# Layer 0 of a two-layer graph-attention kernel: sums by pairs of tiles, masks in two halves, denominators of eight tiles together, with smaller stage and mask rings

## Chip, cores and metric

One NeuronCore of one Trainium2 chip runs the whole kernel. The metric is the device time in microseconds (us) of one execution; the number quoted for a kernel is the median of several runs. A difference of 0.2% (7 us) is about what a measurement of this kernel can tell from none.

## Reference, cut to what matters

`x` is 8192 x 64, `adj` is 8192 x 8192 int32 (0 or 1, about one in a thousand is 1). Three graph-attention passes follow each other; the kernel calls them layers 0, 1 and 2. Each computes, for every row i, a softmax over the columns j at which the mask is set:

```
# layer 0
scores = (x @ W @ a1)[:, None] + (entity @ W @ a2)[None, :]
e      = leaky_relu(scores, 0.2); e = where(adj > 0, e, -9e15)
h      = softmax(e, axis=1) @ entity_embs + x
x      = layernorm(x + elu(h))
# layers 1 and 2 (two steps of the second module, the same mask)
Wh = h @ W_l;  scores = leaky_relu(u + v.T + c);  scores = where(adj > 0, scores, -9e15)
h  = 0.2 * x + 0.8 * elu(softmax(scores, axis=1) @ Wh)
...
out = layernorm(x + concat(x, h1, h2) @ mlp_w + mlp_b)
```

## The kernel before, in words

**Tiling.** The 8192 rows i are handled in 16 blocks (NB) of 512. For a block, the 8192 columns j go by in 64 tiles (NT) of 128: a tile is a 128 x 512 matrix with j on the partitions and the block's rows along the free axis. So each layer is 16 x 64 = 1024 tiles. Layers run one after the other, and within a layer the blocks b and the tiles t are two nested loops, unrolled on every engine.

**One tile, step by step.** (1) A start of the scores is written to one of five PSUM banks (`eps`, ES = 5) by VectorE (DVE), line 1156; in layer 0, 17 of the 64 tiles of a block (the set ON_ACT) are started by ScalarE (ACT) instead, line 564. (2) TensorE (PE) adds the mask: `mask_scores`, line 754, multiplies a diagonal of -9e15 (`nbig`) with the tile of the inverted mask. For tiles started by ACT it also adds a row of bounds (`mrow`, line 751) first. (3) ACT takes exp into a slot of a ring of probabilities, `probs`, line 577. (4) PE adds the slot to two running sums in PSUM: `main` (line 798) multiplies with the 64 features; tile j goes to the upper or lower half of the columns by its parity, so that two tiles run side by side in two 64-column halves of the array. `denominators` (line 807) sums four tiles side by side in four 32-column quarters. Layer 1 needs no denominators: its features carry a column of their difference.

**Order of PE's work.** PE's instructions run in program order. In layers 1 and 2 the unit is a pair of tiles: after the mask of every second tile, `main` of the pair two back (GROUP 2, LAG 2). In layer 2 `two_quads` sums the denominators of eight tiles together, once in eight tiles, at t % 8 = 3 (DEN 8, DLAG 3). In layer 0 the unit is a quad: after the mask of every fourth tile, `sums` runs two `main` and one `denominators` for the quad one back (GROUP 4, LAG 1). `mask_scores` writes in pieces of 32 columns in layer 0 (four instructions that run side by side) and of 64 columns in layers 1 and 2 (MASK_COLS), and in one piece of 128 columns near steps that use the whole array.

**Rings.** The ring `prob` has eight slots (TS). Layer 2 uses 16: eight more lie in the buffer `mi`, which layer 0 needs for mask units and later layers don't. `probs` waits until the slot it writes has been summed.

**Tails and heads.** While block b runs, the end of block b-1 (its tail: the sums out of PSUM at t = 4 and 5, turning, division, elu, layer norm, the products for the next layer) and the start of block b+1 (its head: counting edges by level on PE, the row bounds on DVE, T_XOR, T_HIST, T_HEAD, T_HEADT, T_ROWS) are spread over fixed values of t, written by hand at the top of the file.

**The mask, made in layer 0.** The adjacency comes in 512 units of 128 x 1024 int32 (512 KB), 32 for a block. A unit is loaded by SyncE's (SP) queue into one of five slots of `stage` (SS = 5), line 401, once unit h - SS has been used; DVE compares it and writes bytes to `mi` (line 995); `mi` holds eight pairs of units (MR = 8). Each pair is turned by a DMA transpose into `nt` (line 414), and each eight units are stored for the later layers (line 431). All of these are issued in order by SP, as `unit` has it. 32 units are made before the first tile, 52 in block 0, and 32 in each block from 1 to 13, one for two tiles; the last 12 fall in block 14. DVE's program has the mask unit (`make_mask`) between the starts of the tiles, and waits there, in order, until the unit has landed. Layers 1 and 2 load the stored masks (line 437).

The lines that SP runs for one unit:

```
def unit(h):
    if h + SS < NU:
        adj_load(h + SS)      # waits for mask unit h
    if h % 2 == 1:
        turn(h)               # waits for mask unit h
    if h % MU == 3 and h > MU:
        store(h // MU - 1)
```

Of the kernel before, what the change touches and what calls it, by code (L numbers as in the profile page):

```python
# [6 lines left out]
ACT = mybir.ActivationFunctionType  # L7
F32 = mybir.dt.float32
# [8 lines left out]
P = 128  # L17
N = 8192
C = 64
HID = 32  # L20
CE = C + 1
NT = N // P
BI = 512
RT = BI // P
NB = N // BI
# [3 lines left out]
MU = UNITS // MV  # L29
MT = NT // MV  # L30
NU = NB * UNITS
MR = 8
PRO = UNITS
AFTER = 20
SS = 5
HB = 32
LV = 16
SPACE = 14
# [66 lines left out]
def build(nc, x, adj, ent, W0, a0, W12, lin_w, lin_b, attn, mlp_w, mlp_b, out):  # L105
    with ExitStack() as ctx:
# [6 lines left out]
        def sem(name):  # L113
            return ctx.enter_context(nc.semaphore(name))
# [8 lines left out]
        mi = sb("mi", [P, MR, 2 * CW], U8)  # L123
# [70 lines left out]
        eps = ps("eps", [P, ES, BI])  # L194
        acc = ps("acc", [P, BI])
        den = ps("den", [P, BI])
        more = mi[:, :, :].rearrange("p s w -> p (s w)").bitcast(F32).rearrange("p (s w) -> p s w", w=BI)
        misc = ps("misc", [P, BI])
        miscb = misc[:, :].bitcast(BF16)

# [44 lines left out]
        s_pair = sem("pair_of_probs_summed")  # L245
        s_main = sem("probs_used")
        s_den = sem("probs_in_denominators")

# [37 lines left out]
        def tile(l, b, j):  # L286
            return (l * NB + b) * NT + j
# [25 lines left out]
        def den_blocks(l, b):  # L313

            return b if l == 0 else (l - 1) * NB + b

        def group(l, b, k):

            return sum(NB * (NT // GROUP[i]) for i in range(l)) + b * (NT // GROUP[l]) + k

        def summed(l, b, j):

            if j < 0:
                l, b, j = (l, b - 1, j + NT) if b else (l - 1, NB - 1, j + NT)
            return group(l, b, j // GROUP[l]) + 1

        def started(l, b, j, on_act):

# [208 lines left out]
        def _(act):  # L537
# [28 lines left out]

            def probs(l, b, j):

                if l < 2 and j % GROUP[l] == 0 and not (l == 0 and b == 0 and j < TS):
                    act.wait_ge(s_main, summed(l, b, j - TS + GROUP[l] - 1))  # L570
                if l == 2 and j % DEN == 0:
                    if b == 0 and j < TS:
                        act.wait_ge(s_main, group(2, 0, 0))
                    elif b or j >= 2 * TS:
                        act.wait_ge(s_den, b * (NT // DEN) + j // DEN - 1)
                act.wait_ge(s_z, tile(l, b, j) + 1)
                nc.scalar.activation(weights(l, j), eps[:, j % ES, :], ACT.Exp,  # L577
                                     bias=v2col[:, j:j + 1]).then_inc(s_p, 1)

            def sums_out(l, b, par):  # L580
                if l:
                    act.wait_ge(s_main, group(l, b, NT // GROUP[l]))
                else:
                    act.wait_ge(s_pair, (b + 1) * (NT // QUAD))
                nc.scalar.activation(acc_s[:, :], acc[:, :], ACT.Copy).then_inc(s_acce, 1)  # L585

            def denominators_out(l, b):
                if l:
                    act.wait_ge(s_den, (b + 1) * (NT // DEN))
                else:  # L590
                    act.wait_ge(s_main, group(l, b, NT // GROUP[l]))
# [99 lines left out]
        def _(pe):  # L691
# [36 lines left out]

            def mask_cols(l, j, head, tail):

                n = GROUP[l]
                first = j // n * n - 1
# [7 lines left out]
                return P if any(first <= t < first + n for t in whole) else MASK_COLS[l]  # L740

            def mask_scores(l, b, j, par, cols):

# [46 lines left out]
            def main(l, b, k):  # L790

                for i in range(2):
                    j = 2 * k + i
                    h = C * i
                    pe.wait_ge(s_p, tile(l, b, j) + 1)
                    if j == 0 and not (l == 0 and b == 0):
                        pe.wait_ge(s_acce, blk(l, b))
                    mm = nc.tensor.matmul(acc[h:h + C, :], feat[:, l % 2, j, 0:C], weights(l, j),  # L798
                                          start=(k == 0), stop=(k == NT // 2 - 1))
                return mm  # L800

            def denominators(l, b, k):

                if k == 0 and not (l == 0 and b == 0):
                    pe.wait_ge(s_dene, den_blocks(l, b))
                for i in range(QUAD):
                    mm = nc.tensor.matmul(den[32 * i:32 * i + 32, :], ones[:, 0:32], weights(l, QUAD * k + i),  # L807
                                          start=(k == 0), stop=(k == NT // QUAD - 1))
                return mm

            def sums(l, b, k):

                if l:
                    main(l, b, k).then_inc(s_main, 1)
                else:
                    main(l, b, 2 * k)
                    main(l, b, 2 * k + 1).then_inc(s_pair, 1)
                    denominators(l, b, k).then_inc(s_main, 1)

            def two_quads(b, g):  # L820
                denominators(2, b, 2 * g)
                denominators(2, b, 2 * g + 1).then_inc(s_den, 1)

            def bounds(l):
                pe.wait_ge(s_colm, l + 1)
# [61 lines left out]
            for l in range(NLAYER):  # L887
# [13 lines left out]
                def body(b, par, head, tail):  # L901
                    for t in range(NT):
                        if tail and t == T_HT:
                            pe.wait_ge(s_h, blk(l, b))
                        wait_started(l, b, t)
                        mask_scores(l, b, t, par, mask_cols(l, t, head, tail))
                        if t % GROUP[l] == GROUP[l] - 1:
                            k = t // GROUP[l] - LAG[l]
                            if k >= 0:
                                sums(l, b, k)  # L910
                            elif tail:
                                sums(l, b - 1, NT // GROUP[l] + k)
                        if l == 2 and t % DEN == DLAG:
                            g = t // DEN - 1
                            if g >= 0:
                                two_quads(b, g)
                            elif tail:
                                two_quads(b - 1, NT // DEN + g)
                        if tail:
                            tail_step(l, b - 1, t)  # L920
                        if b == 0 and t < (NT + 2) // 3:
                            if t == 0:
                                pe.wait_ge(s_cbe, blk(l, 0) + 1)
                            for j in range(3 * t, min(3 * t + 3, NT)):
                                feature_sum(l, j)
                        if b == 0 and l == 1 and t == T_FSUM + 3:
                            pe.wait_ge(s_fs1e, 1)
                            nc.tensor.matmul(misc[:, 0:CE], acc_s[0:C, 0:P], turnw[0:C, :], start=True,
                                             stop=True).then_inc(s_fsum, 1)
                        if head and t == T_HIST[0]:  # L930
                            if tail:
                                pe.wait_ge(s_oe, 4 * blk(l, b))
                            else:
                                pe.wait_ge(s_fsume, l + 1)
                        for m in range(MV if head else 0):
                            if t == T_HIST[m]:
                                count_edges(l, b + 1, m)
                        if head and t == T_FOLD:
                            turn_counts(l, b + 1)
                        if head and t == T_HEADT:  # L940
                            turn_maxima(l, b + 1)
                        if head and t == T_ROWS:
                            spread_maxima(l, b + 1, 1 - par)

                blocks(body)
                for k in range(NT // GROUP[l] - LAG[l], NT // GROUP[l]):
                    sums(l, NB - 1, k)
                if l == 2:
                    two_quads(NB - 1, NT // DEN - 1)
# [343 lines left out]
```

## Time and profile before

| | |
|---|---|
| median of three runs | 3500.31 us (3499.39 to 3500.57) |
| profiled execution | 3499.27 us, span 3497.5 us |
| TensorE clock granted, mean | 0.983 of full |
| busy, share of the span | PE 92%, DVE 82%, ACT 65%, POOL 3% |
| DMA | 578.71 MB, 165 GB/s mean over the span |

The busy share of PE counts matmuls; weight loads (PEld) overlap them. "Share" of the DMA is the time of all packets over 16 engines; packets can overlap, so that it can be over 1. The 1.8 us between the span and the execution's own time lie outside the profile. The granted clock has two levels, 1.2 and 2.4 GHz, shown as 0.5 and 1.0.

### The profile page before, as it was taken

What the parts mean: (1) busy time and instruction counts of PE and PEld (TensorE: products, weight loads), DVE (VectorE), ACT (ScalarE), POOL (GpSimd) and SP (SyncE); (2) the same over time, 40 slices, a digit from 0 to 9 for tenths busy, and PEclk for the clock granted to TensorE, in tenths of its full rate; (3) what the DMA queues carried; (4) which work ended last, traced back from release to release, by engine and by line L of the source; (5) the groups of instructions that cost most, each with busy time, mean ns of one, the idle gap of its engine ahead of it and who ended that gap; (6) DMA issues with size and microseconds to landing.
All of it is one profiled execution on the core that took longest, in us unless ns stands there. A gap on an engine that the chain in (4) does not pass through costs nothing. (4 is left out here: it accounts for less than half of the span.)

```text
span 3497.5 us, 58252 instructions
## 1 busy us (share of the span) xinstructions
PE 3203.8 (92%) x22959; PEld 1152.7 (33%) x22959; DVE 2873.2 (82%) x5283; ACT 2269.0 (65%) x3933; POOL 114.3 (3%) x138
## 2 busy tenths in 40 slices
PE   1679999999999999799999999988999999999998
PEld 0323333333333333333333333334333333333333
DVE  5468888888888875699999999986888888888886
ACT  0247766676776666377777787773666666666665
POOL 0000000000000000000000000000000000000000
PEclk9989999999999999899999999998999999999999
DMA  8999999999999951222222222112111211221210
GB/s 253 283 348 346 341 329 347 336 333 340 343 333 341 333 180 54 85 85 97 76 100 73 100 73 101 72 61 85 69 72 64 90 71 57 86 82 57 85 33 7
DMA packets 414116, 578.71 MB, mean 165 GB/s; under 512 B 294402, under 2 KB 315010, under 8 KB 389266
## 3 DMA queue, kind: packets, MB, share of 16 engines
q1 hardware_dynamic: 409458, 564.40, 50.2%
q0 software_dynamic: 4384, 10.59, 1.0%
q8 instruction: 180, 2.95, 0.4%
q14 instruction: 94, 0.77, 0.1%
HBM read 430.10 MB, written 77.69 MB: 145 GB/s over the span
## 5 line engine op out<-in xcount | busy, mean ns | idle before, releaser
L1156 DVE SCALAR_TENSOR_TENSOR eps<-ua,v8col,cb 128x512 f32<-128x512 f32 x2800 | 1971.3, 754 | 376.3 <-ACT prob L577 238.9
L577 ACT ACTIVATE prob<-eps,v2col 128x512 f32<-128x512 f32 x2560 | 1628.4, 688 | 692.2 <-PE eps L754 678.9
L798 PE MATMUL acc<-prob,feat 128*64 128x512 f32 x5120 | 1303.3, 605 | 6.6 <-ACT acc_s L585 6.6
L754 PE MATMUL eps<-nt,nbig 128*64 128x512 fp8e4 (+2 forms) x6542 | 994.3, 384 | 114.4 <-DVE eps L1156 110.4
L754 PEld LDWEIGHTS eps<-nt,nbig 128*64 128x64 bf16 (+2 forms) x6542 | 329.8, 104 | 956.0 <-DVE eps L1156 612.5
L798 PEld LDWEIGHTS acc<-prob,feat 128*64 128x64 f32 x5120 | 326.2, 137 | 397.9 <-issue 215.0
L577 ACT ACTIVATE mi<-eps,v2col 128x512 f32<-128x512 f32 x512 | 328.0, 686 | 156.7 <-PE eps L754 152.7
L995 DVE TENSOR_SCALAR mi<-stage 128x1024 uint8<-128x1024 int32 x512 | 352.2, 689 | 62.9 <-DMA stage<-in_adj_dram 62.5
L807 PE MATMUL den<-prob,ones 128*32 128x512 f32 x3072 | 397.0, 604 | 0.0
L798 PE MATMUL acc<-mi,feat 128*64 128x512 f32 x1024 | 264.8, 597 | 0.0
L1004 DVE TENSOR_SCALAR edges<-nt 128x2048 int32<-128x2048 int32 x192 | 234.2, 1220 | 31.1 <-PE misc L765 16.3
L765 PE MATMUL misc<-edges,oneh 128*32 128x512 fp8e4 x3072 | 190.8, 390 | 70.6 <-DVE edges L1004 55.8
L564 ACT ACTIVATE eps<-ub,v8col 128x512 f32<-128x512 f32 x272 | 189.4, 696 | 0.0
L807 PEld LDWEIGHTS den<-prob,ones 128*32 128x32 f32 x3072 | 67.1, 108 | 301.0 <-issue 301.0
L765 PEld LDWEIGHTS misc<-edges,oneh 128*32 128x32 bf16 x3072 | 85.0, 98 | 198.3 <-issue 81.1
L807 PE MATMUL den<-mi,ones 128*32 128x512 f32 x1024 | 123.1, 598 | 0.0
L751 PE MATMUL eps<-mrow,onesb 128*32 128x512 bf16 (+1 forms) x800 | 106.5, 379 | 0.0
L633 ACT ACTIVATE hs<-misc 128x512 f32<-128x512 f32 x48 | 28.3, 589 | 93.8 <-PE misc L765 93.8
L798 PEld LDWEIGHTS acc<-mi,feat 128*64 128x64 f32 x1024 | 68.2, 137 | 54.4 <-issue 20.2
L878 PEld LDWEIGHTS misc<-wcat,ht 65*128 65x128 f32 x384 | 52.5, 198 | 77.8 <-issue 49.5
L637 ACT ACTIVATE mrow<-misc 3x512 bf16<-3x512 bf16 x48 | 28.1, 586 | 76.3 <-PE misc L841 76.3
L878 PE MATMUL misc<-wcat,ht 65*128 65x130 f32 (+1 forms) x384 | 69.8, 306 | 6.5 <-ACT pj L624 4.5
(159 smaller groups left out, 1407.1 us busy)
## 6 DMA issues: line engine op xcount, KB each, us to landing
stage<-in_adj_dram SPq DMA_DIRECT2D x512, 512.0 KB, 6.5
nt<-nt_d SPq DMA_DIRECT2D x128, 1024.0 KB, 5.2
nt_d<-nt SPq DMA_DIRECT2D x64, 1024.0 KB, 7.2
ub<-u_d SPq DMA_DIRECT2D x48, 256.0 KB, 5.2
xy_d<-xin POOLq DMA_DIRECT2D x32, 256.0 KB, 3.3
xin<-xy_d SPq DMA_DIRECT2D x32, 256.0 KB, 2.9
nt<-mi SPq DMA_TRANSPOSE x256, 7.2
xin<-in_x_dram SPq DMA_DIRECT2D x16, 128.0 KB, 6.3
```

The lines of the kernel that those rows point to most:

```text
L564: nc.scalar.activation(eps[:, j % ES, :], ub[:, par, :], ACT.Relu, bias=v8col[:, j:j + 1], scale=1.0 - ALPHA).then_inc(s_filla, 1)
L577: nc.scalar.activation(weights(l, j), eps[:, j % ES, :], ACT.Exp, bias=v2col[:, j:j + 1]).then_inc(s_p, 1)
L633: nc.scalar.activation(hs[:, :], misc[:, :], ACT.Copy).then_inc(s_hse, 1)
L751: nc.tensor.matmul(et[c:c + cols, :], onesb[:, c:c + cols], mrow[:, par, :], start=False, stop=False, skip_group_check=True, tile_position ...
L754: mm = nc.tensor.matmul(et[c:c + cols, :], nbig[:, c:c + cols], edge, start=False, stop=True, skip_group_check=True, tile_position=(0, c))
L765: mm = nc.tensor.matmul(misc[s * HB:(s + 1) * HB, :], oneh[:, m * MT + j, :], half_block(edges[:, n % 2, :], m, j), start=(m == 0 and k == 0),
L798: mm = nc.tensor.matmul(acc[h:h + C, :], feat[:, l % 2, j, 0:C], weights(l, j), start=(k == 0), stop=(k == NT // 2 - 1))
L807: mm = nc.tensor.matmul(den[32 * i:32 * i + 32, :], ones[:, 0:32], weights(l, QUAD * k + i), start=(k == 0), stop=(k == NT // QUAD - 1))
L878: mm = nc.tensor.matmul(misc[:, r * WC + w:(r + 1) * WC], ht[:, (2 * i + r) * P:(2 * i + r + 1) * P], wcat[:, l, w:WC], start=True, stop=True)
L995: dv.tensor_scalar(out, src, 0, ONE8, ALU.is_le, ALU.mult).then_inc(s_mask, 1)
L1004: dv.tensor_scalar(edges[:, n % 2, :].bitcast(I32), nt[:, b % 2, m, :].bitcast(I32), EDGE_FLIP, None, ALU.bitwise_xor).then_inc(s_xor, 1)
L1156: dv.scalar_tensor_tensor(eps[:, j % ES, :], ua[:, par, :], v8col[:, j:j + 1], cb[:, par, :], ALU.add, ALU.max).then_inc(s_fill, 1)
```

## The change

In layer 0 `mask_scores` writes in pieces of 64 columns (HALF); `main` runs by pairs with a lag of two pairs; `denominators` runs for eight tiles together, as in layer 2. The ring of probabilities has 12 slots of its own in all layers (TS = 12), counted over all tiles of the kernel, and layer 2 no longer uses `mi`. ACT's wait for a free slot stands before every second tile, in every layer; in layer 0 and 2 it is for the denominators, in layer 1 for `main`. To make room, `mi` has six pairs in place of eight (MR) and `stage` four slots in place of five (SS).

```
-MR = 8
+MR = 6
-SS = 5
+SS = 4
-GROUP = (QUAD, 2, 2)
-LAG = (1, 2, 2)
+PAIRLAG = 2
-TS = 2 * QUAD
-SLOTS = (TS, TS, 2 * TS)
+TS = 3 * QUAD
-MASK_COLS = (32, 64, 64)
+HALF = 64
...
-        def weights(l, j):
-            n = j % SLOTS[l]
-            return prob[:, n, :] if n < TS else more[:, n - TS, :]
+        def weights(l, b, j):
+            return prob[:, tile(l, b, j) % TS, :]
...
             def probs(l, b, j):
-                if l < 2 and j % GROUP[l] == 0 and not (l == 0 and b == 0 and j < TS):
-                    act.wait_ge(s_main, summed(l, b, j - TS + GROUP[l] - 1))
-                if l == 2 and j % DEN == 0:
-                    if b == 0 and j < TS:
-                        act.wait_ge(s_main, group(2, 0, 0))
-                    elif b or j >= 2 * TS:
-                        act.wait_ge(s_den, b * (NT // DEN) + j // DEN - 1)
+                if tile(l, b, j) >= TS and j % 2 == 0:
+                    old, i = divmod(tile(l, b, j) - TS, NT)
+                    ol, ob = divmod(old, NB)
+                    if ol == 1:
+                        act.wait_ge(s_main, pairs(ol, ob, i // 2 + 1))
+                    else:
+                        act.wait_ge(s_den, dens(ol, ob, i // DEN + 1))
                 act.wait_ge(s_z, tile(l, b, j) + 1)
...
-                        if t % GROUP[l] == GROUP[l] - 1:
-                            k = t // GROUP[l] - LAG[l]
+                        if t % 2 == 1:
+                            k = t // 2 - PAIRLAG
                             if k >= 0:
-                                sums(l, b, k)
+                                main(l, b, k).then_inc(s_main, 1)
                             elif tail:
-                                sums(l, b - 1, NT // GROUP[l] + k)
-                        if l == 2 and t % DEN == DLAG:
+                                main(l, b - 1, NT // 2 + k).then_inc(s_main, 1)
+                        if l != 1 and t % DEN == DLAG:
                             g = t // DEN - 1
                             if g >= 0:
-                                two_quads(b, g)
+                                two_quads(l, b, g)
```

## Rows read from the trace of the kernel before

**Rows 1.** Windows: stretch, length, busy PE, PEld, DVE, ACT, POOL, clock, DMA share, GB/s.

```profile
126.00:249.00 123.00, 99.97 (x681) 43.07 (x685) 79.45 (x129) 55.46 (x90) 0.00 (x0) 0.90 1.07 337
249.08:325.43 76.35, 73.14 (x600) 24.52 (x592) 65.11 (x123) 53.59 (x97) 3.26 (x3) 1.00 1.11 341
325.43:1247.03 921.60, 883.01 (x7156) 295.91 (x7157) 783.61 (x1477) 642.80 (x1140) 35.17 (x36) 1.00 1.11 338
1247.03:1322.08 75.05, 73.67 (x604) 24.84 (x606) 52.40 (x101) 53.33 (x96) 2.82 (x3) 1.00 0.43 132
1322.08:1388.24 66.16, 65.97 (x537) 21.49 (x530) 37.44 (x68) 48.96 (x88) 2.81 (x3) 1.00 0.11 43
...
2458.00:3405.00 947.00, 944.62 (x6678) 336.35 (x6670) 799.74 (x1506) 611.30 (x1026) 36.54 (x28) 1.00 0.19 69
```

**Rows 2.** ACT's copy that opens each block (t = 4), 325 to 1248 us.

```profile
L585 ACT ACTIVATE acc_s<-acc x13: 597/597/597, 325.4 to 1247.0; 128x512 f32<-128x512 f32 x13
```

**Rows 3.** ACT's copy that opens each block, layer 2.

```profile
L585 ACT ACTIVATE acc_s<-acc x14: 597/597/598, 2472.9 to 3348.7; 128x512 f32<-128x512 f32 x14
```

**Rows 4.** Groups by line, one layer 0 block: busy, mean ns | idle before.

```profile
L1156 DVE SCALAR_TENSOR_TENSOR eps<-ua,v8col,cb 128x512 f32<-128x512 f32 x47 | 34.8, 755 | 8.3 <-ACT prob L577 8.0
...
L995 DVE TENSOR_SCALAR mi<-stage 128x1024 uint8<-128x1024 int32 x33 | 22.7, 689 | 0.0
...
L754 PE MATMUL eps<-nt,nbig 128*32 128x512 fp8e4 x160 | 12.8, 381 | 2.7 <-DVE eps L1156 2.6
```

**Rows 5.** Timeline of PE in layer 0, away from tail and head.

```profile
643.09 0.40 PE L751 MATMUL eps<-mrow,onesb 128*32 128x512 bf16 x4
643.31 1.23 PE L754 MATMUL eps<-nt,nbig 128*32 128x512 fp8e4 x16
644.47 1.94 PE L798 MATMUL acc<-prob,feat 128*64 128x512 f32 x8
...
647.22 0.40 PE L751 MATMUL eps<-mrow,onesb 128*32 128x512 bf16 x4
...
651.38 0.59 PE L754 MATMUL eps<-nt,nbig 128*32 128x512 fp8e4 x5
```

**Rows 6.** Timeline of PE in layer 2, away from tail and head.

```profile
2467.38 0.62 PE L754 MATMUL eps<-nt,nbig 128*64 128x512 fp8e4 x4
...
2472.66 1.92 PE L807 MATMUL den<-mi,ones 128*32 128x512 f32 x16
2474.52 0.62 PE L754 MATMUL eps<-nt,nbig 128*64 128x512 fp8e4 x4
```

**Rows 7.** Timeline of PE in layer 0, near the head (tiles 51 to 54).

```profile
616.72 0.40 PE L754 MATMUL eps<-nt,nbig 128*32 128x512 fp8e4 x4 [0.91 <-DVE eps L1156]
```

**Rows 8.** Who waited for whom, layer 0 without its first blocks.

```profile
DVE mi L995 <- DMA stage<-in_adj_dram: 0.4, 1, 0.4
```

**Rows 9.** Who waited for whom, block 0.

```profile
DVE mi L995 <- DMA stage<-in_adj_dram: 34.4, 21, 5.1
```

**Rows 10.** DMA in 145 to 198 us (block 0): total, and the loads' issues.

```profile
DMA packets 16105, 18.86 MB, mean 356 GB/s; under 512 B 12567, under 2 KB 12567, under 8 KB 15717
...
stage<-in_adj_dram SPq DMA_DIRECT2D x23, 512.0 KB, 7.0
```

**Rows 11.** DMA in 60 to 100 us (before the first tile).

```profile
DMA packets 13714, 15.15 MB, mean 379 GB/s; under 512 B 10912, under 2 KB 10912, under 8 KB 13458
...
stage<-in_adj_dram SPq DMA_DIRECT2D x20, 512.0 KB, 6.3
```

**Rows 12.** DMA in 859 to 936 us (a steady block).

```profile
DMA packets 23276, 26.03 MB, mean 338 GB/s; under 512 B 18465, under 2 KB 18469, under 8 KB 22757
...
stage<-in_adj_dram SPq DMA_DIRECT2D x32, 512.0 KB, 6.4
```

**Rows 13.** The loads of the adjacency, 327 to 1100 us: time to landing.

```profile
DMA to landing us min/median/max: 3.8/6.5/10.2
```

**Rows 14.** The DMA transposes of the mask, whole kernel: time that one holds SP.

```profile
L414 SPq DMA_TRANSPOSE nt<-mi x256: 1231/2330/5803, 36.5 to 1267.4; - x128
```

More of the change, by code:

```diff
@@ L196, in build @@
         den = ps("den", [P, BI])
-        more = mi[:, :, :].rearrange("p s w -> p (s w)").bitcast(F32).rearrange("p (s w) -> p s w", w=BI)
         misc = ps("misc", [P, BI])
@@ L244, in build @@
         s_p = sem("probs_done")
-        s_pair = sem("pair_of_probs_summed")
         s_main = sem("probs_used")
@@ L315, in den_blocks, with pairs, dens @@
             return b if l == 0 else (l - 1) * NB + b
[L317 to L325, printed above, removed]
+        def pairs(l, b, n):
+            return (l * NB + b) * (NT // 2) + n
+        def dens(l, b, n):
+            return den_blocks(l, b) * (NT // DEN) + n
         def started(l, b, j, on_act):
@@ L567, in probs @@
             def probs(l, b, j):
-                if l < 2 and j % GROUP[l] == 0 and not (l == 0 and b == 0 and j < TS):
-                    act.wait_ge(s_main, summed(l, b, j - TS + GROUP[l] - 1))
-                if l == 2 and j % DEN == 0:
-                    if b == 0 and j < TS:
-                        act.wait_ge(s_main, group(2, 0, 0))
-                    elif b or j >= 2 * TS:
-                        act.wait_ge(s_den, b * (NT // DEN) + j // DEN - 1)
+                if tile(l, b, j) >= TS and j % 2 == 0:
[5 more added lines that the diff above has]
+                        act.wait_ge(s_den, dens(ol, ob, i // DEN + 1))
                 act.wait_ge(s_z, tile(l, b, j) + 1)
-                nc.scalar.activation(weights(l, j), eps[:, j % ES, :], ACT.Exp,
+                nc.scalar.activation(weights(l, b, j), eps[:, j % ES, :], ACT.Exp,
                                      bias=v2col[:, j:j + 1]).then_inc(s_p, 1)
             def sums_out(l, b, par):
[L581 to L584, printed above, removed]
+                act.wait_ge(s_main, pairs(l, b, NT // 2))
                 nc.scalar.activation(acc_s[:, :], acc[:, :], ACT.Copy).then_inc(s_acce, 1)
             def denominators_out(l, b):
[L588 to L591, printed above, removed]
+                act.wait_ge(s_den, dens(l, b, NT // DEN))
                 nc.scalar.activation(den_s[:, :], den[:, :], ACT.Copy).then_inc(s_dene, 1)
@@ L729, in mask_cols @@
             def mask_cols(l, j, head, tail):
-                n = GROUP[l]
-                first = j // n * n - 1
+                first = j // 2 * 2 - 1
                 whole = []
@@ L739, in mask_cols @@
                     whole += [T_FOLD, T_HEADT, T_ROWS]
-                return P if any(first <= t < first + n for t in whole) else MASK_COLS[l]
+                return P if any(first <= t < first + 2 for t in whole) else HALF
             def mask_scores(l, b, j, par, cols):
@@ L797, in main @@
                         pe.wait_ge(s_acce, blk(l, b))
-                    mm = nc.tensor.matmul(acc[h:h + C, :], feat[:, l % 2, j, 0:C], weights(l, j),
+                    mm = nc.tensor.matmul(acc[h:h + C, :], feat[:, l % 2, j, 0:C], weights(l, b, j),
                                           start=(k == 0), stop=(k == NT // 2 - 1))
@@ L806, in denominators, with two_quads @@
                 for i in range(QUAD):
-                    mm = nc.tensor.matmul(den[32 * i:32 * i + 32, :], ones[:, 0:32], weights(l, QUAD * k + i),
+                    mm = nc.tensor.matmul(den[32 * i:32 * i + 32, :], ones[:, 0:32], weights(l, b, QUAD * k + i),
                                           start=(k == 0), stop=(k == NT // QUAD - 1))
                 return mm
[L811 to L822, printed above, removed]
+            def two_quads(l, b, g):
+                denominators(l, b, 2 * g)
+                denominators(l, b, 2 * g + 1).then_inc(s_den, 1)
             def bounds(l):
@@ L906, in body @@
                         mask_scores(l, b, t, par, mask_cols(l, t, head, tail))
-                        if t % GROUP[l] == GROUP[l] - 1:
-                            k = t // GROUP[l] - LAG[l]
+                        if t % 2 == 1:
+                            k = t // 2 - PAIRLAG
                             if k >= 0:
-                                sums(l, b, k)
+                                main(l, b, k).then_inc(s_main, 1)
                             elif tail:
-                                sums(l, b - 1, NT // GROUP[l] + k)
-                        if l == 2 and t % DEN == DLAG:
+                                main(l, b - 1, NT // 2 + k).then_inc(s_main, 1)
+                        if l != 1 and t % DEN == DLAG:
                             g = t // DEN - 1
                             if g >= 0:
-                                two_quads(b, g)
+                                two_quads(l, b, g)
                             elif tail:
-                                two_quads(b - 1, NT // DEN + g)
+                                two_quads(l, b - 1, NT // DEN + g)
                         if tail:
@@ L945, in _ @@
                 blocks(body)
[L946 to L949, printed above, removed]
+                for k in range(NT // 2 - PAIRLAG, NT // 2):
+                    main(l, NB - 1, k).then_inc(s_main, 1)
+                if l != 1:
+                    two_quads(l, NB - 1, NT // DEN - 1)
                 for t in range(NT):
```

## The prediction, made before the changed kernel ran

> **What bounds the kernel now.** I read the windows first, one for each kind of stretch [rows 1]. The reader should compare the busy columns with the length. Layer 0 from 325.4 to 1247.0 us is twelve blocks (13 copies that open a block [rows 2]), so 76.80 us each. PE is busy for 883.0 of 921.6 us (96%), DVE for 783.6 (85%), ACT for 642.8 (70%), and the DMA share is 1.11. Layer 2 does nearly the same arithmetic in 875.8 / 13 = 67.37 us a block [rows 3], with PE at 99.7% and the DMA at 0.19 [rows 1]. So PE sets the pace now, but in layer 0 two others are close behind: DVE, which also makes the mask, and the DMA, which brings 32 units a block. That the DMA keeps up is seen in the waits: in 773 us DVE waited for a landed unit once, for 0.4 us [rows 8]. In block 0, where 52 units are due in one block, it waited 21 times for 34.4 us [rows 9], and the block takes 123 us between copies [rows 1]. There the DMA is the bound.
>
> **Part 1: PE's order.** Away from tail and head, two quads of layer 0 go from 643.09 to 651.38 = 8.29 us [rows 5]; they hold eight masks and three rows of bounds, each row one more step of 643.31 - 643.09 = 0.22 us. Layer 2's eight tiles by pairs go from 2467.38 to 2474.52 = 7.14 us [rows 6] with no such row. The changed layer 0 should have 7.14 + 3 x 0.22 = 7.80, a gain of 0.49 in eight tiles and 3.9 in 64: 76.8 - 3.9 = 72.9 us a block. The number of products is the same; what goes is the gap at each change of column width. Before, masks (32 columns), `main` (64) and denominators (32) change width twice in four tiles; afterwards twice in eight.
>
> The Trainium skill (TensorEngine Tiling (Array Packing), Key Properties) says that changing the tiling mode drains TensorE. By that rule alone the number of drains halves, from 32 to 16 in a block; the page gives no price for one.
>
> From below, the block is bounded by layer 2's own plus 17 bound rows: 67.37 + 17 x 0.22 = 71.1. From above it is bounded by what DVE holds back: masks in layer 0 stood 2.7 us a block waiting for a start by DVE [rows 4], for instance 0.91 us near the head [rows 7], and that stall does not shrink when PE gets faster; it may grow. DVE would be 65.3 / 73 = 89% busy, with its starts (755 ns) and mask units (689 ns) in one queue [rows 4]. I add 0.6 for it: **73.5 us by PE and DVE**.
>
> **Part 2: the DMA, asked to run faster.** Nothing is taken off it: a block moves 26.03 MB [rows 12]. What it can do when it is the bound is shown twice. In block 0, 23 loads in 53 us at 356 GB/s [rows 10]: 2.30 us a unit, 73.7 us for 32. Before the first tile, 20 loads in 40 us at 379 GB/s [rows 11]: 2.00 us a unit, 64 us for 32, with the engines almost idle. I take 73.7, the stretch that has exp, masks and sums beside it. So the DMA's floor lies right at PE's new pace: most of what PE gains is just allowed, and no more.
>
> The Trainium skill (SBUF — State Buffer, SBUF: two separate sides) says "A DMA cannot be slowed by a compute op". By that rule the 379 GB/s would hold in a block too, the floor would be 26.03 / 0.379 = 68.7 us, and the block would stay at PE's 73.5. The trace so far doesn't agree (356 beside the engines against 379 without them); it gives the first rival below.
>
> **Part 3: the smaller rings.** SP issues load h + 4 once mask unit h is used, no longer h + 5. At 2.4 us a unit the old ring gave a load 5 x 2.4 - 0.69 = 11.3 us from issue to need; the slowest landing was 10.2, the median 6.5 [rows 13], hence no waits. At 2.33 us a unit the new one gives 4 x 2.33 - 0.69 = 8.6, less the time in which SP is held by a transpose ahead of it in its queue (median 2.3 us, at most 5.8 [rows 14]). So the median load still lands in time and the slow ones come a microsecond or two late. DVE waits for them in program order, and behind them stand the starts of scores, on which PE's masks wait, with at most five banks of lead; also the transposes, which wait on the mask. The price per block lies between 0 (the lead covers all) and tens of us (block 0's 34.4 [rows 9]). I take 1.1, near the low end, since the median fits: **74.6 us a block**. In block 0 and before it, where the DMA already is the bound, a shorter queue can only lose: 0 to 12 us, I take 2% of 123 = 2.5, and 1.5 for one unit fewer landed when DVE comes to the masks (a unit is 2.0 [rows 11]). MR = 6 I cost at nothing: a pair's slot comes round after six pairs, 28 us, against landings of some 7; if SP fell behind, it would add to the same wait.
>
> **Part 4: ring and waits of the probabilities, at nothing.** With 12 slots, tile 8g + 12 waits for the denominators of tiles 8g to 8g + 7. PE runs those before mask 8g + 12, which the same exp needs anyway. So no new wait ends last, in layer 0 or layer 2; in layer 1 `main` of the slot ran seven tiles earlier. In layer 2 ACT meets a wait before every second tile, not every eighth: 24 more a block. ACT is busy for 611 of 947 us there [rows 1], which covers them; were ACT the bound there, they would count in full. The copy of the sums now comes after the last pair, as in layer 2, before the next `main`.
>
> **Sum**, against the profiled execution (3499.3 us; its span 3497.5 and 1.8 us around it; the median of the runs is 1.0 higher):
> - twelve blocks: 12 x (76.8 - 74.6) = 26.4
> - the block before them: 76.35 - 74.6 = 1.8
> - 1247 to 1322 us, with twelve units at its beginning alone (DMA share 0.43 [rows 1]): 3.5, part 1 without the DMA
> - the last block, 66.16 us with PE at 99.7% [rows 1]: 3.4, seven of eight groups
> - block 0 and before: -2.5 - 1.5
> - layers 1 and 2: 0
>
> Together 31.1: 3499.3 - 31.1 = **3468 us**.
>
> **The rivals.**
> *The DMA gives way* (0.27). In steady blocks it is not waited for, so its floor there may be lower than block 0's; then blocks come to PE's 73.5, and at best 71.1. 13 x 3.3 + 6.9 - 1 = 49: 3450 us; with 71.1 and all else at its best, 3418. For it: 379 GB/s was reached. Against it: the share is 1.11 in steady blocks and 1.07 where the DMA is the bound [rows 1], so it looks no less full.
> *The DMA holds at the old pace* (0.13). If 338 GB/s [rows 12] is all it has in a steady block, 26.03 / 0.338 = 77.0 us and no block gets shorter; only the last two gain: 3499 - 6.9 + 4 = 3496, within 0.2%. Against it: block 0 ran at 356.
> *The stage ring starves DVE* (0.20), slower. Place: DVE's wait for the landed unit, every block from 0 to 13. In block 0 five slots went round in 5 x 2.30 = 11.5 us. If that time is latency and SP's queue rather than bandwidth, four slots need up to 2.88 us a unit, 92 us a block. It decides from 2.4 us a unit upwards (76.8 / 32). At a middle value, 2.5, a block takes 80.0: 13 x 3.2 + 6 - 7 = 41 us slower, 3540. Against it: landing 7.0 and mask 0.7 make 7.7, so four slots could go round in 1.9 us a unit if SP's delay went away with the queue.
> *The forecast* has 0.40. That the change doesn't do what it says is no case of its own: the same code runs layer 2 at the pace used here.
>
> **How the numbers follow.** The likeliest case gives 3468, by itself 3455 to 3488. The range goes down into the first rival, 3430, leaving out its best end, and up to 3515, leaving out most of the starved case: about 0.1 on each side. A measurement of this kernel tells 0.2% (7 us) from none. Faster by more: 0.40 + 0.27 and a little of the others, 0.69. Within it: 0.13. Slower: 0.18.
>
> **What would show each step.** In eight quiet tiles of layer 0 PE should take 7.8 us, with one group of 16 `den` products. The period of the opening copies should be 74.6 with DVE's wait for the stage at 1 to 3 us a block. If that wait stays near 0 and the period is 73.5 or less, the DMA had room; if it is over 5 us a block, the ring or the DMA is the bound, and which one is told by the GB/s: the ring if they fall below 338. Layers 1 and 2 should keep their 67.37 us and their times. A period over 76.8, or any change in layer 2, would make the prediction wrong.

## The result, and the profile after

Before: 3499.08 us, the median of eight runs (3497.71 to 3500.57). Changed: 3489.68 us, the median of eight (3486.48 to 3499.82). The ratio of the two is 0.9977, with a 95% interval of 0.9966 to 0.9988: the change makes the kernel 0.2% faster, 9 us, where 31 us were forecast. The profiled execution has a span of 3486.5 us, 11.0 less than before.

The windows of the changed kernel, cut as [rows 1] were, by its own opening copies (columns: stretch, length, busy time of PE, its weight loads, DVE, ACT and POOL, granted clock, DMA share, GB/s):

```profile
246.61:324.42 77.81, 72.45 (x505) 25.25 (x509) 64.75 (x124) 54.68 (x96) 3.34 (x3) 1.00 1.09 345
324.42:1241.44 917.02, 867.25 (x6016) 302.77 (x6054) 778.55 (x1477) 653.14 (x1141) 39.69 (x36) 1.00 1.10 338
1241.44:1314.62 73.18, 71.62 (x509) 25.68 (x512) 52.98 (x102) 53.88 (x96) 2.82 (x3) 1.00 0.45 147
1314.62:1378.46 63.84, 63.71 (x424) 22.50 (x422) 37.01 (x68) 49.18 (x89) 2.81 (x3) 1.00 0.14 56
2450.00:3395.00 945.00, 939.59 (x6644) 334.33 (x6659) 795.75 (x1500) 613.52 (x1024) 36.56 (x28) 1.00 0.19 70
```

The opening copies of the twelve steady blocks, against [rows 2]:

```profile
L575 ACT ACTIVATE acc_s<-acc x13: 597/598/603, 324.4 to 1241.4; 128x512 f32<-128x512 f32 x13
```

And those of layer 2, against [rows 3]:

```profile
L575 ACT ACTIVATE acc_s<-acc x14: 596/596/599, 2460.9 to 3337.6; 128x512 f32<-128x512 f32 x14
```

The twelve blocks take 917.0 / 12 = 76.42 us each, 0.38 less than before; 74.6 was forecast. PE is busy for 867.3 us of them, 15.8 less than in [rows 1], yet its idle time grew from 38.6 to 49.8. Layer 0 ends 9.8 us earlier in all (the last window ends at 1378.46, before at 1388.24): 2.5 by the first copy (246.6 against 249.1), less 1.5 in the next block (77.81 against 76.35), 4.6 in the twelve, 1.9 in the block after them, 2.3 in the last. Layer 2 has 876.7 / 13 = 67.44 us a block and is as it was.

Who waited for whom, from 327 to 1100 us as in [rows 8]:

```profile
DVE mi L972 <- DMA stage<-in_adj_dram: 58.7, 38, 4.5
...
PE eps L740 <- DVE eps L1133: 39.5, 73, 1.7
```

DVE's wait for a landed unit, 0.4 us before, is now 58.7 us in 38 places, some 5.8 us a block. How one of them reaches PE is seen at tiles 40 to 47 of a block, first on DVE:

```profile
515.32 0.70 DVE L972 TENSOR_SCALAR mi<-stage 128x1024 uint8<-128x1024 int32 x1 [3.88 <-DMA stage<-in_adj_dram]
```

and then on PE:

```profile
513.92 1.02 PE L784 MATMUL acc<-prob,feat 128*64 128x512 f32 x4
514.78 0.60 PE L740 MATMUL eps<-nt,nbig 128*64 128x512 fp8e4 x4
515.21 1.02 PE L784 MATMUL acc<-prob,feat 128*64 128x512 f32 x4
...
516.28 0.38 PE L740 MATMUL eps<-nt,nbig 128*64 128x512 fp8e4 x2
517.87 0.41 PE L740 MATMUL eps<-nt,nbig 128*64 128x512 fp8e4 x2 [1.20 <-DVE eps L1133]
...
519.66 0.41 PE L740 MATMUL eps<-nt,nbig 128*64 128x512 fp8e4 x2 [0.53 <-DVE eps L1133]
520.93 0.41 PE L740 MATMUL eps<-nt,nbig 128*64 128x512 fp8e4 x2 [0.86 <-DVE eps L1133]
...
522.12 1.92 PE L793 MATMUL den<-prob,ones 128*32 128x512 f32 x16
```

Where nothing is late, a pair takes 1.29 us (513.92 to 515.21), as in layer 2, and the denominators of eight tiles are one group of 16. From 516.28 to 520.93 PE stands three times, 1.20, 0.53 and 0.86 us, for the start of the next tile. DVE stood for 3.88 us until 515.32, because a unit had not landed, and then had that mask unit and two edge units of 1.2 us between the starts. The regular cadence of before is gone too: single blocks take from 74.2 to 79.7 us, where twelve before had 76.8 each.

A stretch of eight tiles in which DVE is never late shows what the order does for PE itself:

```profile
872.37 0.41 PE L737 MATMUL eps<-mrow,onesb 128*64 128x512 bf16 x2
...
876.70 0.38 PE L740 MATMUL eps<-nt,nbig 128*64 128x512 fp8e4 x2
877.07 0.41 PE L737 MATMUL eps<-mrow,onesb 128*64 128x512 bf16 x2
...
880.33 0.62 PE L740 MATMUL eps<-nt,nbig 128*64 128x512 fp8e4 x4
```

880.33 - 872.37 = 7.96 us for eight tiles and three rows of bounds, 0.15 of them a pause before 877.07 that no mark shows (the step is 0.37 us there, otherwise 0.22). Without it they are 7.81, and 7.8 was forecast.

### The profile page after: what moved, and what is told of

Read it like the earlier page. It is cut to its first block and busy times, and to the rows that moved or that the text cites. A ratio compares the mean times of both kernels' runs of the same rounds, so it can differ in the third digit from the quotient of the medians.

```text
span 3486.5 us, 55844 instructions
## 1 busy us (share of the span) xinstructions
PE 3172.4 (91%) x21396; PEld 1157.8 (33%) x21477; DVE 2865.1 (82%) x5283; ACT 2288.1 (66%) x3933; POOL 118.9 (3%) x138
## 5 line engine op out<-in xcount | busy, mean ns | idle before, releaser
L570 ACT ACTIVATE prob<-eps,v2col 128x512 f32<-128x512 f32 x3072 | 1968.3, 688 | 863.8 <-PE eps L740 845.1
L784 PE MATMUL acc<-prob,feat 128*64 128x512 f32 x6144 | 1601.7, 601 | 6.4 <-ACT acc_s L575 6.4
L740 PE MATMUL eps<-nt,nbig 128*64 128x512 fp8e4 (+1 forms) x5382 | 1022.5, 386 | 142.7 <-DVE eps L1133 137.1
L740 PEld LDWEIGHTS eps<-nt,nbig 128*64 128x64 bf16 (+1 forms) x5382 | 329.0, 109 | 1076.9 <-DVE eps L1133 693.8
L784 PEld LDWEIGHTS acc<-prob,feat 128*64 128x64 f32 x6144 | 403.3, 137 | 312.6 <-issue 122.1
L793 PE MATMUL den<-prob,ones 128*32 128x512 f32 x4096 | 492.9, 599 | 0.0
L737 PE MATMUL eps<-mrow,onesb 128*64 128x512 bf16 (+1 forms) x445 | 92.9, 385 | 2.4 <-issue 2.4
L1048 DVE SCALAR_TENSOR_TENSOR g<-fsum,emp,misc 128x65 f32<-128x65 f32 x192 | 40.9, 275 | 25.1 <-PE misc L838 20.2
L760 PEld LDWEIGHTS misc<-fold,hs 128*128 128x128 f32 x384 | 47.3, 194 | 40.5 <-issue 36.5
L509 POOL TENSOR_TENSOR rstd<-mom,half 128x4 f32<-128x4 f32 x16 | 23.1, 1444 | 1094.3 <-DVE mom L1037 1094.3
L519 POOL TENSOR_TENSOR rstd<-mom,half 128x4 f32<-128x4 f32 x16 | 23.0, 1435 | 1052.5 <-DVE mom L1037 1052.5
```

Of the source, the lines that this page charges most:

```text
L570: nc.scalar.activation(weights(l, b, j), eps[:, j % ES, :], ACT.Exp, bias=v2col[:, j:j + 1]).then_inc(s_p, 1)
L737: nc.tensor.matmul(et[c:c + cols, :], onesb[:, c:c + cols], mrow[:, par, :], start=False, stop=False, skip_group_check=True, tile_position ...
L740: mm = nc.tensor.matmul(et[c:c + cols, :], nbig[:, c:c + cols], edge, start=False, stop=True, skip_group_check=True, tile_position=(0, c))
L760: mm = nc.tensor.matmul(misc[:, r * HB:(r + 1) * HB], hs[:, r * P:(r + 1) * P], fold[:, :], start=True, stop=True)
```

## The experiments

Three questions: what do PE and DVE allow in the new order, what does the ring of the stage cost, and what the DMA's bandwidth? The steady block of layer 0 is the measure, from the first to the last of 13 opening copies, so that 12 blocks lie between. Every run with lightened loads is a single execution; it is read by its blocks, which agree with each other to 0.02 us in all of them.

**With halved loads, before and after.** The stage is set to zero once, and a load brings only half of its columns; the mask is then not the whole adjacency, but every instruction of the engines stays.

```
-sp.dma_start(stage[:, h % SS, :], adj_v[b, 2 * m + c, r])
+sp.dma_start(stage[:, h % SS, 0:CW // 2], adj_v[b, 2 * m + c, r][:, 0:CW // 2])
```

> The kernel before, with each load of the adjacency halved: only the first 512 of a unit's 1024 columns are loaded, the rest of the stage is set to zero once and stays so (so the mask is not the whole adjacency; all instructions of the engines stay). It shows the pace of layer 0 without the DMA as a bound. If PE's order bounds the old kernel, its steady blocks in layer 0 keep 76.8 us (76.3 to 76.9). If the DMA bounds it, they fall below 76. Block 0 falls from 119 us to under 90 in either case.

> The changed kernel with the same halved loads. My theory: what PE and DVE allow is 73.5 us a block (forecast, 72.9 to 74.5), and the DMA or the stage ring takes the rest of the 76.4 that the changed kernel has; DVE's wait for the stage is near 0. Rival, that the new order itself is slow in layer 0 (DVE between its mask units and the starts): the blocks stay at 76 us or more even so.

Opening copies of the kernel before with halved loads:

```profile
L585 ACT ACTIVATE acc_s<-acc x13: 597/597/598, 295.3 to 1216.9; 128x512 f32<-128x512 f32 x13
```

Of the changed kernel with halved loads:

```profile
L575 ACT ACTIVATE acc_s<-acc x13: 597/597/599, 294.5 to 1182.3; 128x512 f32<-128x512 f32 x13
```

921.6 / 12 = 76.80 us: the old kernel does not gain a hundredth from a DMA with much less to do, so PE's order, with its waits for DVE, was the whole of its pace. Block 0, from PE's first mask to the first copy, fell from 122.8 to 100.7 us, not under 90 as I had expected: the DMA was only a part of what made it long. The changed one has 887.8 / 12 = 73.98, and DVE waits for no unit in it. So the new order is worth 2.8 us a block, and 2.44 of them are lost again in the changed kernel. Single executions took 3469.1 and 3429.0 us; the 40 us between them are what the order would bring with a DMA that is never late.

Of the 2.8 us, PE's idle time (the length less its busy time) is 1.6: it falls from 921.60 - 877.50 = 44.1 to 887.75 - 862.44 = 25.3 us in the twelve blocks. The other 1.2 are shorter work of PE, to which the next runs give a reason.

**What is left in the 74.0.** In the first, the mask units of DVE are halved too (with halved loads); in the second, the masks are in pieces of 32 columns, so that the array changes width at every pair; in the third, the old quads have masks of 64.

```
+out, src = out[:, 0:2], src[:, 0:2]        # light_after_dve, in make_mask
-HALF = 64
+HALF = 32                                  # light_after_m32
-MASK_COLS = (32, 64, 64)
+MASK_COLS = (64, 64, 64)                   # light_before_m64
```

> The changed kernel with halved loads, and DVE's mask units write only the first two of four groups (half of the work of each; the rest of the mask buffer is set once). PE's own work of a block is 71.1 by layer 2 plus the bound rows; DVE's mask units are held to be what makes 74.0 of it. Then blocks fall to 71.1 to 72. If PE's tail and head of layer 0 are themselves longer, they stay at 73 to 74.

> The changed kernel with halved loads and with masks in pieces of 32 columns in all layers, sums by pairs as they are. If the change of column width costs PE time, it now changes twice per pair of tiles and not twice in eight: blocks of layer 0 go from 74.0 to 77 to 80, of layer 2 from 67.4 to 70 to 73, of layer 1 from 56.9 to 60. If the gain of the order came from elsewhere (fewer waits), they stay within 0.5 us.

> The kernel before with halved loads and with masks in layer 0 in pieces of 64 columns in place of 32, its quads as they are. The array then changes width as often as before: masks and main at 64, denominators at 32, twice in four tiles. If the number of changes is what counts, the blocks stay at 76.8 (76.5 to 77.1); if four small matrix products beside each other cost more than two, they fall to 75 to 76.

The opening copies in layer 0 of the first:

```profile
L575 ACT ACTIVATE acc_s<-acc x13: 610/614/615, 298.7 to 1167.5; 128x512 f32<-128x512 f32 x13
```

of the second, in layer 0 and in layer 2:

```profile
L575 ACT ACTIVATE acc_s<-acc x13: 600/604/606, 295.2 to 1205.0; 128x512 f32<-128x512 f32 x13
```

```profile
L575 ACT ACTIVATE acc_s<-acc x14: 597/597/599, 2544.0 to 3479.4; 128x512 f32<-128x512 f32 x14
```

and of the third:

```profile
L585 ACT ACTIVATE acc_s<-acc x13: 597/597/599, 294.4 to 1212.7; 128x512 f32<-128x512 f32 x13
```

Mask units of half the size: 868.8 / 12 = 72.40. It was to be 71.1 to 72. DVE is busy for 7.9 us a block less, and that gives back 1.6 of the 2.9 us above the lower bound; what its mask units cost in all is more than that, if anything, since half of each is still there. PE is still idle for 0.9 us a block in this run (868.8 - 857.8 = 11.0 in twelve), so some 0.4 of the other 1.3 are PE's own work, which the bound of 71.1 had too low.

Masks of 32 columns: 75.82 in layer 0, below the 77 to 80 that I expected; 935.4 / 13 = 71.95 in layer 2 and 706.8 / 12 = 58.90 in layer 1, within what I expected. Layer 2, where PE is never short of work, is the clean case: 4.5 us a block. Counted product by product in the traces, a block of layer 2 changes the width 33 times, and 69 times with these masks. These are 36 more and not 48 (six more in each eight tiles), since near the tail and the head the masks are 128 columns wide in either run. So one change costs 4.5 / 36 = 0.125 us. A quiet pair of that run says the same:

```profile
2563.83 1.08 PE L784 MATMUL acc<-prob,feat 128*64 128x512 f32 x4
...
2565.38 1.08 PE L784 MATMUL acc<-prob,feat 128*64 128x512 f32 x4
```

It takes 1.55 us where it took 1.29, for two changes more. In layer 0 part of the cost hides behind DVE. The quads with masks of 64: 918.3 / 12 = 76.53, 0.3 less with a hundred products fewer in a block; the changes are 42 a block, as in the kernel before. So the number of changes counts, and the number of pieces hardly.

How many changes the order takes away is then a matter of counting: a block of layer 0 has 42 before and 36 after, six fewer, not the sixteen of the prediction. (The pieces of 128 columns are also chosen by pairs of tiles now and not by quads, which the description of the change leaves out.) Six changes are 0.75 us. With the 1.6 us of idle time they make 2.3 of the 2.8; the last 0.5 I can't name.

**The stage ring, alone and given back.**

```
-SS = 5
+SS = 4          # before_ss4, nothing else of the change
```

> The kernel before with four stage slots in place of five, nothing else. If the ring starves DVE (it makes the DMA slower, not only its queue shorter), steady blocks go from 76.8 to 78 to 80 us, the time to about 3515 to 3545, and DVE waits for the stage 3 to 6 us a block. If only the DMA's bandwidth counts, they stay at 76.8 to 77.2 and the time within 0.2% (3492 to 3506), block 0 included.

Its copies, and DVE's wait for the stage from 327 to 1100 us:

```profile
L585 ACT ACTIVATE acc_s<-acc x13: 597/597/598, 332.2 to 1267.1; 128x512 f32<-128x512 f32 x13
```

```profile
DVE mi L995 <- DMA stage<-in_adj_dram: 44.6, 44, 3.8
```

934.9 / 12 = 77.91 us a block, 1.1 more than before; the time is 3518.7 us, a ratio of 1.0056 (1.0041 to 1.0071), close to the lower end of what I expected if the ring starves DVE. So the fifth slot was worth 19 us to the old kernel too, though DVE had shown no wait there. The first copy falls 4.9 us later.

To give it back to the changed kernel, room must be found. The first try took two probability slots:

```
-TS = 3 * QUAD
+TS = 10
-SS = 4
+SS = 5
```

> The changed kernel with five stage slots again; the room comes from two probability slots (ten in place of twelve, so that the exp of tiles 8g + 10 and 8g + 11 waits for the denominators of the eight before). Ring theory: blocks fall from 76.4 to about 74.5, the time to 3455 to 3470. Bandwidth theory: 76 us a block and no gain, 3485 to 3495; with the shorter probability ring costing anything, more.

```profile
L575 ACT ACTIVATE acc_s<-acc x13: 596/597/598, 327.7 to 1263.9; 128x512 f32<-128x512 f32 x13
```

```profile
ACT prob L570 <- PE den L793: 227.1, 80, 3.5
```

78.0 us a block, ratio 1.0219 (1.0202 to 1.0236) and 3575.8 us in all, and DVE doesn't wait for the stage any more. But ACT waits 227 us for the denominators of eight, some 23 a block: with ten slots, the exp of two tiles in eight can't run before them. In layer 2 the same costs 3.8 us a block. This told nothing of the stage at the pace of 74; it shows that the twelve slots are needed. The second try took the room elsewhere: weights used in the setup alone lie in the last probability slots, and two index tensors over a buffer of the head.

```
-        w0row = sb("w0row", [P, 2, C])
+        w0row = prob[:, 10, 132:132 + 2 * C].rearrange("p (s c) -> p s c", s=2)
-        wt = sb("wt", [C, NLAYER, CE])
+        wt = prob[0:C, 11, 0:NLAYER * CE].rearrange("f (l c) -> f l c", l=NLAYER)
...
-        kk = sb("kk", [P, NT], I32)
+        kk = he[:, 0:2, :].rearrange("p r k -> p (r k)")
...
-SS = 4
+SS = 5
```

> The changed kernel with five stage slots and all twelve probability slots; the room comes from small tensors of the setup that now lie in the probability ring's last slots before it is used, and from two index tensors laid over a buffer of the head. Two theories for the 2.4 us a block between the changed kernel's 76.4 and the 74.0 that it has with halved loads. Ring: the fourth slot is too few, and the fifth gives back most of it; blocks 74.2 to 75, time 3458 to 3472. Bandwidth: the DMA moves no more than some 340 GB/s beside the engines whatever the ring; blocks 75.8 to 76.4 and time 3480 to 3488.

```profile
L576 ACT ACTIVATE acc_s<-acc x13: 597/597/599, 325.6 to 1226.4; 128x512 f32<-128x512 f32 x13
```

```profile
DVE mi L973 <- DMA stage<-in_adj_dram: 27.7, 34, 1.8
```

The DMA from 400 to 1000 us:

```profile
DMA packets 181709, 206.01 MB, mean 343 GB/s; under 512 B 143351, under 2 KB 143383, under 8 KB 177687
```

900.8 / 12 = 75.07 us a block, and 3472.3 us in all, a ratio of 0.9923 (0.9908 to 0.9938) to the kernel before. The time lies just above my 3458 to 3472, the blocks just above 75. DVE's wait falls from 58.7 to 27.7 us, and the DMA moves 343 GB/s in place of 337. So the ring took 76.42 - 75.07 = 1.35 of the 2.44 us, and neither theory holds alone.

**The last 1.1 us: a sixth slot, or fewer bytes.**

```
-MR = 6
-SS = 4
+MR = 4
+SS = 6                                     # after_ss6, with the room of after_ss5
```

```
-sp.dma_start(stage[:, h % SS, :], adj_v[...])
+sp.dma_start(stage[:, h % SS, 0:CW * 7 // 8], adj_v[...][:, 0:CW * 7 // 8])   # light78_after_ss5
```

> The changed kernel with six stage slots and all twelve probability slots; the mask pairs' ring goes from six to four for it. With five slots the blocks take 75.1 us, with halved loads 74.0. If the queue's length is still what is missing, a sixth slot brings them to 74.0 to 74.5 and the time to 3458 to 3466. If the last microsecond is the DMA's bandwidth, they stay at 74.8 to 75.2 and the time at 3468 to 3475. The shorter ring of mask pairs is held to cost nothing.

> The changed kernel with five stage slots, and loads of 896 of a unit's 1024 columns (the rest of the stage is set once and stays zero; the engines do all their work). That takes 2.1 MB of some 26 off a block, 8%. If the 1.1 us a block between 75.1 (five slots) and 74.0 (halved loads) is the DMA's bandwidth, nearly all of it goes: 74.0 to 74.3. If it is latency or the order of SP's queue, the blocks stay at 74.8 to 75.1.

Copies with six slots, and DVE's wait from 327 to 1100 us:

```profile
L576 ACT ACTIVATE acc_s<-acc x13: 597/597/600, 319.3 to 1223.0; 128x512 f32<-128x512 f32 x13
```

```profile
DVE mi L973 <- DMA stage<-in_adj_dram: 53.8, 52, 3.7
```

Copies, and the window over the same twelve blocks, with five slots and loads of seven eighths:

```profile
L576 ACT ACTIVATE acc_s<-acc x13: 597/597/600, 314.2 to 1202.0; 128x512 f32<-128x512 f32 x13
```

```profile
314.22:1202.04 887.82, 865.94 (x6052) 304.20 (x6054) 778.86 (x1477) 650.52 (x1141) 39.72 (x36) 1.00 1.10 321
```

A sixth slot gives the blocks nothing (903.7 / 12 = 75.31), and DVE waits longer, 53.8 us in 52 places, of which the blocks show 0.24 us at most. The run also has a shorter ring of mask pairs, which I did not run apart. Its time is 3469.7 us, ratio 0.9915 (0.9901 to 0.9928), with the interval overlapping that of five slots. With an eighth less to load, the blocks take 887.8 / 12 = 73.98, to a hundredth what they take with halved loads. So the rest, 75.07 - 73.98 = 1.1 us, goes with the bytes. A smaller load also lands sooner (median 5.6 us against 7.3), but the time to landing isn't it: a sixth slot allows for more of it and brings nothing, while the median is 7.3 us with either ring and the DMA moves 343 and 344 GB/s. So it is the rate at which the DMA moves them. What holds the rate there I have not taken apart.

**Two tries to go on.** One makes the mask 16 units ahead in place of 20, the other moves one of DVE's edge units.

```
-AFTER = 20
+AFTER = 16                                 # after_lead16, four stage slots
-T_XOR = (29, 32, 40, 41)
+T_XOR = (29, 32, 37, 41)                   # after_ss5_xor, five stage slots
```

> The changed kernel with the mask made 16 units ahead of a block in place of 20 (so 48 units in block 0 and not 52, and 16 in place of 12 left for block 14, where the DMA has room). Block 0 is DMA bound at some 2.3 us a unit, so four units fewer should take 9 us off it (7 to 10); the blocks after it keep 76.4, block 14 may take 1 to 2 us more. Time 3479 to 3484 against 3490 for the changed kernel. Rival: the edges' counting, whose chunks then land nearer to their use, waits; then blocks grow by a microsecond or more and the time stays at 3490 or rises.

> The changed kernel with five stage slots, and the third of DVE's four edge units of a block moved from tile 40 to tile 37, in all layers. In the changed kernel tiles 40 to 47 of layer 0 take 12.8 us, 1.9 more than with halved loads: two edge units of 1.2 us one after the other on DVE leave it no lead when a load is late. Apart from each other they should cost 0.3 to 0.8 us a block less: time 3460 to 3468 against 3472. Rival: the load that is late holds DVE wherever the edge units stand; then 3470 to 3474.

The first: in block 0, DVE's edge units wait for a turned chunk:

```profile
DVE edges L981 <- DMA nt<-mi: 8.4, 1, 8.4
```

3487.4 us, ratio 0.9967 (0.9953 to 0.9981), no gain that stands clear of the changed kernel's own 0.9977; I had expected 3479 to 3484. The last of the 32 units of block 1 is now made at tile 41 of block 0, where the edges of its chunk are due, so 8.4 us are waited for at once. DVE's waits for the stage in that stretch did fall, from 37.3 to 28.8 us, and the one wait takes that back. The second: in 327 to 1100 us, DVE now waits for PE's count of the chunk two before:

```profile
DVE edges L982 <- PE misc L752: 33.3, 10, 3.4
```

3520.0 us, ratio 1.0060 (1.0046 to 1.0074): 48 us slower than with five slots alone, where I had expected a gain of 4 to 12. Ten waits of some 3.3 us stand in ten blocks of layer 0, which take 75.7 us (75.07 with five slots alone). Layer 1 takes 57.9 us a block (56.9) and layer 2 69.0 (67.4), with the same wait in them. DVE runs some tiles ahead of PE, and at its tile 37 PE has not yet counted, at tile 35, what stands in the buffer that DVE wants. Both were misses of mine, and both for the same reason: a fixed place in one engine's program is not a time.

**The best version** of the study is the changed kernel with five or six stage slots, 3472.3 and 3469.7 us: 27 to 30 us faster than the kernel before, and 17 to 20 faster than the changed one.

## Why the prediction was wrong

The sign was right, 31 us were forecast and 9 came. In the profiled execution it is 11.0 of 31.1, and by the terms of the sum the 20 us are: the twelve blocks 21.8 short (76.42 us each, not 74.6), the block before them 3.3 (it lost 1.5 and was to gain 1.8), the last two 2.7. Against that, block 0 and what is before it gained 2.5 us where a loss of 4.0 was forecast, and 1.2 lie behind layer 0. I have no reason for either, so that part of the miss is hidden by luck. The 1.82 us of a steady block are 0.48 in part 1, 1.09 in part 2 and 0.25 in part 3:

- **Part 1, the order (73.5 forecast, 73.98 measured with halved loads).** A change of width has a cost, as the forecast had it; the drains that the Trainium skill speaks of (TensorEngine Tiling (Array Packing), Key Properties) show as 0.125 us for each change in layer 2. But there are six fewer in a block and not sixteen, 0.75 us. I also took the two quads' 8.29 us [rows 5] for PE's own work: the first row of 16 products hides a pause of 0.18 us (its step is 1.16 us; the four masks of the second quad take 0.98 besides their row of bounds). The quiet gain is 8.29 - 7.96 = 0.33 us in eight tiles, not 0.49. That the gain of a block, 2.8 us, lies near eight times that is in part luck, since 1.6 of it is idle time of PE that went, and part 1 had held that this stall would not shrink. Part of the difference to 71.1 is DVE's mask units, as forecast: at least 1.6 us. Mis-sized by 0.48 in all.
- **Part 2, the DMA.** This is the step that failed. I found the DMA's floor at 73.7 and PE's pace at 73.5, and put the DMA into the sum at nothing: 74.6 is 73.5 and the 1.1 of part 3. With five slots, so without the loss by the ring, the DMA cost 1.09 us (75.07 against 73.98), and an eighth fewer bytes took all of it away. The floor itself was wrong. It was worked out from 356 GB/s in 53 us of block 0 [rows 10]; over 600 us of steady blocks the DMA moved 343 GB/s with five slots and 344 with six, while DVE still waited for it. By [rows 1] a block is 338 GB/s x 76.80 us = 25.96 MB, which takes some 75.6 us at that rate: within a per cent of the 75.07 and 75.31 that came, and 2 us above 73.7. That this is the DMA's limit there, and not just what it was asked for, is my reading; for it speaks that a sixth slot changed neither rate nor period, and that the period fell as soon as there were fewer bytes. Why block 0 had 356 stays open.
- **Part 3, the smaller ring.** 1.1 us forecast, 1.35 measured (76.42 against 75.07), and 1.1 in the old kernel alone. The size was near; the rival of a starved DVE, 2.5 us a unit, did not come: 76.42 / 32 = 2.39. Before and in block 0 I expected 4 us of loss. The first copy came 2.5 us earlier in the changed kernel, and 4.9 later with the ring alone, near the 4.0 of the sum. What made up for it in the changed kernel I have not settled. Block 0 was also less of a DMA stretch than I took it for: it still takes 100.7 us with halved loads.
- **The rule on the ports.** The Trainium skill (SBUF — State Buffer, SBUF: two separate sides) would have a DMA not slowed by compute, and gave the rival of 3450 us. The DMA moved 338 GB/s in the changed kernel's blocks, as before, 344 with six slots (both rows stand in this document), and never the 379 of [rows 11]. That alone doesn't refute the rule, since the mix of transfers and the waits in SP's queue are different there too, and no run changed only the work of the engines beside whole loads; but its consequence for this kernel, that the 379 are to be had, was not seen in any run.
- **Part 4, layers 1 and 2 at nothing.** Right: 67.44 us a block in layer 2 with the twelve slots and the waits at every second tile. The run with ten slots shows that this was no matter of course.
- **The last two blocks.** 3.5 and 3.4 us forecast, 1.9 and 2.3 measured, by the same over-sized part 1.

The rival "the DMA holds at the old pace" (3496) came nearest, in time and in rate: the DMA did 338 GB/s. I gave it 0.13, since I read block 0's 356 GB/s as what a steady block could have. It is right in kind only: 338 GB/s was not all that the DMA had, with a fifth slot it moved 343.

The DMA of 400 to 1000 us in the changed kernel with six slots, and the loads' time to landing in the changed kernel, which answers to [rows 13]:

```profile
DMA packets 182570, 206.23 MB, mean 344 GB/s; under 512 B 144211, under 2 KB 144243, under 8 KB 178547
```

```profile
DMA to landing us min/median/max: 3.5/6.4/9.6
```

With four slots the landing didn't get slower (median 6.4, at most 9.6); it is the time allowed for it that got shorter. With five and six slots the median is 7.3 us at 343 and 344 GB/s: more loads are under way at once and each takes longer, at nearly the same rate.

## What to carry to other kernels

Take the rate of a bound from a stretch like the one that it will be used for. Here 53 us of block 0 gave a floor of 73.7 us, just beside PE's pace, and the rate of the steady blocks with five or six slots gives some 75.6; an eighth fewer bytes, and PE's pace of 73.98 us was met to a hundredth. When two bounds come out that near to each other, a run with one of them lightened tells them apart; it is the first experiment to make. Before taking a slot from a ring because nothing waits at it, run the old kernel with that ring shortened; here it cost 19 us by itself and would have shown the price. Before multiplying the gain of a quiet stretch by the length of a block, count in the trace how often the thing that it saves occurs; here it was 6 times and not 16. And look for room in what is used only at the start: some 3 KB a partition, most of it tensors of the setup, were worth 17 us.

## What the runs showed that I had not expected

- A DMA share of 1.10 to 1.11 in steady blocks says nothing of how near the bound is: it is 1.10 with loads of seven eighths too, where DVE waits for no unit any more, and PE and DVE pace the block to a hundredth.
- A ring without a single visible wait (0.4 us in 773) still had no slot to spare: one fewer gave 44.6 us of waits in 44 places.
- A probability ring two slots short cost 3.0 us a block in layer 0 (78.0 against 75.07) and 3.8 in layer 2, the two layers that sum denominators by eight.
